# Gathers of routed rows a tile sooner, uncleared sums, and a reordered opening in a fused feedforward, attention, feedforward kernel

## The reference

```python
x = x + 0.5 * ffn(layernorm(x), ...)
x = x + attention(layernorm(x), Wk, Wq, Wv, Wo, bo)
x = x + 0.5 * ffn(layernorm(x), ...)      # the same weights again
```

## Time and profile before

| | us |
|---|---|
| median of 3 runs | 1111.91 |
| lowest and highest run | 1110.63, 1115.58 |
| profiled execution, its own time | 1111.67 |
| span of the profiled execution | 1109.9 |
| PE, DVE, ACT, POOL busy in it | 1065.2, 739.2, 552.7, 534.1 |

### The profile page before, as it was taken

How to read it: one execution, slowest core, us unless ns; L and a number is a source line. 1 busy time by engine, 2 the same in 40 slices (tenths; PEclk the granted TensorE clock), 3 DMA queues, 4 the chain that set the end, 5 groups by cost and what they waited for, 6 DMA issues and landing times.

```text
span 1109.9 us, 29561 instructions
## 1 busy us (share of the span) xinstructions
PE 1065.2 (96%) x11263; PEld 847.4 (76%) x11264; DVE 739.2 (67%) x1392; ACT 552.7 (50%) x920; POOL 534.1 (48%) x746
## 2 busy tenths in 40 slices
PE   8999999999999989999999999999999999999996
PEld 6788887888876767767767776768888877888864
DVE  5736766677654686877878778756347666767752
ACT  4344335666654456455456365343443355666641
POOL 5720554676665553462552541326201826666652
PEclk9999999999999999999999999999999999999999
DMA  7273035232224210000000000105241152422232
GB/s 267 76 265 154 19 128 178 71 127 70 74 91 143 91 57 3 3 4 2 3 3 3 2 4 3 41 2 211 90 174 39 53 186 71 132 69 70 67 111 79
DMA packets 41172, 89.77 MB, mean 81 GB/s; under 512 B 5844, under 2 KB 30551, under 8 KB 40032
## 3 DMA queue, kind: packets, MB, share of 16 engines
q1 hardware_dynamic: 30416, 62.68, 15.9%
q0 software_dynamic: 10368, 25.19, 7.3%
q10 hardware_dynamic: 272, 0.26, 0.1%
HBM read 65.04 MB, written 26.21 MB: 82 GB/s over the span
## 4 chain that ended last, share of the span: by engine, by line
PE 73%; DVE 13%; ACT 5%; issue 4%; DMA 2%; POOL 2%; DVEq 0%; ACTq 0%; POOLq 0%
PE PS L2018 14%; PE PS L1929 11%; PE PS L2032 9%; PE PS L1945 7%; PE PS L2025 3%; PE PS L2157 3%; PE PS L1860 2%; PE PS L2044 2%; PE PS L2277 2%; PE PS L2290 2%; DVE A_NM L941 2%; PE PS L1963 2%; ACT XNT L1434 1%; PE PS L2311 1%; DVE A_NM L948 1%
## 5 line engine op out<-in xcount | busy, mean ns | idle before, releaser
L2018 PE MATMUL PS<-WHL,XGH 128*128 128x512 f32 x528 | 183.4, 429 | 0.6 <-DVE WHL L802 0.6
L1763 POOL TENSOR_TENSOR A_W<-A_XC,CB 128x256 f32<-128x256 f32 x86 | 61.5, 734 | 156.0 <-DVE A_XC L1046 155.8
L2032 PE MATMUL PS<-WD,XNT 128*128 x528 | 127.2, 384 | 0.6 <-DVE HSB L861 0.6
L1330 ACT ACTIVATE XNT<-PS,SCORES 128x512 f32<-128x512 f32 x72 | 49.6, 688 | 143.2 <-PE PS L2018 127.0
L1663 POOL TENSOR_SCALAR XNTR<-WD 128x128 fp32r<-128x128 f32 x64 | 53.8, 859 | 129.5 <-DVE WD L667 129.5
L1669 POOL DMA_INDIRECT X<-xs_dram,WHO x72 | 90.6, 1259 | 46.6 <-issue 20.2
L2018 PEld LDWEIGHTS PS<-WHL,XGH 128*128 128x128 f32 x528 | 94.7, 190 | 17.5 <-issue 1.5
L1945 PE MATMUL PS<-SDH,HHL 128*128 128x256 f32 x512 | 103.4, 286 | 3.7 <-DVE X L730 3.6
L2032 PEld LDWEIGHTS PS<-WD,XNT 128*128 128x128 f32 x528 | 95.5, 190 | 13.8 <-issue 2.5
L2018 PE MATMUL PS<-WHL,XGL 128*128 128x512 f32 x264 | 104.7, 397 | 0.0
L1291 ACT CAST HHL<-HSB 128x512 fp32r<-128x512 f32 x64 | 39.7, 620 | 111.6 <-PE PS L1945 62.8
(11 more groups left out here) (312 smaller groups left out, 2613.0 us busy)
## 6 DMA issues: line engine op xcount, KB each, us to landing
xs_dram<-WG SPq DMA_DIRECT2D x16, 512.0 KB, 3.0
WU<-in_r_up SPq DMA_DIRECT2D x2, 4096.0 KB, 14.0
shared_dram<-X SPq DMA_DIRECT2D x16, 512.0 KB, 3.3
WG<-in_r_gate SPq DMA_DIRECT2D x2, 4096.0 KB, 17.9
WD<-in_r_down SPq DMA_DIRECT2D x4, 2048.0 KB, 7.7
X<-in_x SPq DMA_DIRECT2D x7, 512.0 KB, 9.3
X<-mid_dram SPq DMA_DIRECT2D x7, 512.0 KB, 3.8
X<-in_r_gate SPq DMA_DIRECT2D x6, 512.0 KB, 3.7
```

Source lines behind the costliest of these rows:

```text
L1330: act.activation(B["RS"][:, u * F:(u + 1) * F], banks[1 + u % 2][:], ACT.Silu, scale=B["SCORES"][:, bass.ds(t if tile is None else tile, 1 ...
L1763: pool.tensor_tensor(B["W"][:].rearrange("p (a m) -> p a m", m=M)[:, part, :], B["XC"][b % 2][:].rearrange("p (a w) -> p a w", w=XW)[:, pa ...
L2018: ins = pe.matmul(banks[bank][:], tok, w[:, k * F:(k + 1) * F], start=(k == 0 and i == 0), stop=(k == KD - 1 and i == 2))
L2032: ins = pe.matmul(banks[7][:, 0:D], B["HT"][:, u * F + f * P:u * F + (f + 1) * P], B["WD"][:, bass.ds(ex * (KF * D) + f * D, D)], start=(f ...
```

## The change

In the order of the code:

- `STATS_SLOT` of feedforward 0: the statistics of group 2 move from slot 0 to slot 1.
- The warm-up has 10 products in place of 8, and three more follow the turn of the first rows.
- DVE makes the low part of the shared up weights before the low parts of the first tokens, and the low part of the down weights in slot 0, after the multiplication, in place of ahead of slot 0.
- In slot 2 of feedforward 0, PE's down products come before the turn of group 1.
- In slot 28 the table is read before the low part of the hidden rows, and in the same slot the numbers of the first two experts are read earlier on DVE and ACT.
- The sums' buffer `RY` is not cleared; POOL waits for the last low part of the shared hidden rows (`hl`) in place of the clearing.
- In the routed loops DVE and ACT read one expert number at the head and one in each tile, in place of four at the head.
- POOL gathers tile 5's rows ahead of the first residual gathers, and from then on tile t + 5's rows where it gathered tile t + 4's.
- In the attention's opening, POOL normalises `S2` of batch 0 before it adds the biases, and adds batch 1's bias in the loop's first step; PE fills with 8 products in place of 3, and makes the second quarter of the maxima's scores ahead of the turned scores.

```diff
@@ -180,7 +180,7 @@
                    ht_sb=SLOT_TILES, ry_ready=SLOT_TILES, ry=SLOT_TILES, ry_out0=16 * TILES3, ry_out1=16 * TILES3, ry_out2=16 * TILES3, wg=16 + 16 * UNR, wu=16 + 16 * UNR, wd=32 + 16 * UNR,
-                   x_out=16 * PARTS_G, x_out_last=16 * (NG - PARTS_G), ry_clear=1, res_in0=16 * TILES3, res_in1=16 * TILES3, res_in2=16 * TILES3)
+                   x_out=16 * PARTS_G, x_out_last=16 * (NG - PARTS_G), res_in0=16 * TILES3, res_in1=16 * TILES3, res_in2=16 * TILES3)
     s = {k: sem(f"ffn_{k}") for k in FFN_PER}
@@ -208,7 +208,7 @@
     SEEDS = (1, FFN_PER["seed"])
-    STATS_SLOT = [{0: 2, 2: 3, 3: 4, 4: 5, 5: 6, 7: 7}, {3: 7}]
+    STATS_SLOT = [{1: 2, 2: 3, 3: 4, 4: 5, 5: 6, 7: 7}, {3: 7}]
     TURN_SLOT = {1: 2, 2: 4, 3: 6, 4: 8, 5: 9, 6: 10, 7: 11}
@@ -217,7 +217,7 @@
     TABLE_SLOT = 28
-    WARM = 8
+    WARM, WARM_TURNED = 10, 3
     GATE_BANK, UP_BANK = (0, 5), (1, 6)
@@ -563,13 +563,11 @@
                 dve.tensor_copy(SUH[:], SU).then_inc(s_split_up, 1)
-                first_low(n)
                 wait_alone(s_split_up, 1)
                 dve.tensor_tensor(SUL[:], SU, SUH[:].bitcast(F32), ALU.subtract).then_inc(s_split_up, 1)
+                first_low(n)
                 dve.wait_ge(s_x[1], 16)
                 stats(1, n)
-                dve.wait_ge(s_split_hi, 2)
-                dve.tensor_tensor(SDL[:], SD, SDH[:].bitcast(F32), ALU.subtract).then_inc(s_split_up, 1)

@@ -735,6 +733,9 @@
                     dve.tensor_tensor(hidden, hidden, banks[UP_BANK[f % 2]][:], ALU.mult).then_inc(s["h"], 1)
+                    if n == 0 and slot == 0:
+                        dve.wait_ge(s_split_hi, 2)
+                        dve.tensor_tensor(SDL[:], SD, SDH[:].bitcast(F32), ALU.subtract).then_inc(s_split_up, 1)
                     if n == 1 and slot == 0:
@@ -743,6 +744,10 @@
                         low_tile(0, 0)
+                    if slot == ROUTING_SLOT["read_table"]:
+                        read_table()
+                    if last and f == 0:
+                        ex.extend(expert(u) for u in range(2))
                     need(dve, "hh", g * KF + f + 1)
@@ -759,7 +764,6 @@
                             need(dve, "wu", 16)
-                            ex.extend(expert(u) for u in range(2))
                         low_weights(*(("WG", ex[0], 0, 0), ("WU", ex[0], 1, 1), ("WG", ex[1], 2, 2))[f])
@@ -789,8 +793,6 @@
                         find_experts()
-                    elif slot == ROUTING_SLOT["read_table"]:
-                        read_table()

@@ -848,8 +850,8 @@
                 low_weights("WU", ex[u + 1], 2 * t + 3, (2 * u) % 3)
-                if first:
-                    dve.memset(B["RY"][:], 0.0).then_inc(s["ry_clear"], 1)
+                if len(ex) < u + 3:
+                    ex.append(expert(t + 2))
                 if not first:
@@ -869,7 +871,7 @@
             with dve.Fori(1, TILES3 - UNR) as it:
-                ex = [None] + [expert(it * UNR + u) for u in range(1, UNR + 2)]
+                ex = [None, expert(it * UNR + 1)]
                 for u in range(UNR):
@@ -1285,6 +1287,9 @@
                         xgt(0, 0)
+                    if last and f == 0:
+                        need(act, "expert_of", 1)
+                        ex.extend(expert(u) for u in range(2))
                     need(act, "h", slot + 1)
@@ -1299,9 +1304,7 @@
                             need(act, "wu", 16)
-                            need(act, "expert_of", 1)
                             need(act, "x_out", 16 * PARTS_G)
-                            ex.extend(expert(u) for u in range(2))
                         high_weights(*(("WG", ex[0], 0), ("WU", ex[0], 1), ("WG", ex[1], 2))[f])
@@ -1686,19 +1691,19 @@
                 gather(u, u)
-            for u in range(2):
+            for u in range(UNR):
                 need("xg_t", u + 1)
                 gather(UNR + u, u)
+            need("hl", KF * NG)
             need("x_out", 16 * PARTS_G)
             need("x_out_last", 16 * (NG - PARTS_G))
-            need("ry_clear", 1)
             for u in range(UNR - 1):
...
                 u, ahead = t % UNR, t + UNR - 1
-                if 0 < t < SLOT_TILES - UNR - 1:
-                    need("xg_t", t + 2)
-                    gather(t + UNR + 1, (t + 1) % UNR)
+                if 0 < t < SLOT_TILES - UNR - 2:
+                    need("xg_t", t + 3)
+                    gather(t + UNR + 2, (t + 2) % UNR)
                 scatter(t, u)
@@ -1792,15 +1797,16 @@
             batch_normalise(1)
+            s2_normalise(0)
             add_bias(0)
-            add_bias(1)
-            s2_normalise(0)
             batch_root(2)
...
                 old, nxt, far, ln = b - 1, b + 1, b + 2, b + 3
+                if b == 0:
+                    add_bias(1)
                 if exists(far):
@@ -1868,10 +1874,13 @@

+            def zeros(times):
+                for _ in range(times):
+                    pe.matmul(banks[7][:, 0:NT * E], B["OH"][:, 0:P], B["OH"][:], start=True, stop=True)
+
             if n == 0:
                 pe.wait_ge(s["nobody"], 1)
-                for _ in range(WARM):
-                    pe.matmul(banks[7][:, 0:NT * E], B["OH"][:, 0:P], B["OH"][:], start=True, stop=True)
+                zeros(WARM)
                 pe.wait_ge(s_const, 16)
@@ -1904,6 +1913,7 @@
                 first_turn(n)
+                zeros(WARM_TURNED)

@@ -1977,6 +1987,9 @@
                     project(NG - 1, 1, 2)
+                turn_behind = n == 0 and slot == 2
+                if turn_behind:
+                    shared_down(0, 0)
                 if slot in turns:
@@ -1995,7 +2008,7 @@
                     xt(0, 0)
-                if slot >= 2:
+                if slot >= 2 and not turn_behind:
                     shared_down((slot - 2) // KF, (slot - 2) % KF)
@@ -2354,7 +2367,7 @@
             turn(1, 1)
-            fill(1, 3)
+            fill(1, 8)
             pe.wait_ge(att["s3m"], count("s3m", 0, 4))
@@ -2365,11 +2378,11 @@
             project_qk(1, 0)
+            pe.wait_ge(att["s1m"], count("s1m", 0, 1))
+            first_s1_max(1)
             pe.wait_ge(s_picks, 5)
...
             s3_turned(0, 0)
-            pe.wait_ge(att["s1m"], count("s1m", 0, 1))
-            first_s1_max(1)
             project_qk(1, 1)
```

## The result

| | before | after |
|---|---|---|
| median of the runs, us | 1111.91 (five, 1105.38 to 1115.58) | 1102.55 (five, 1098.29 to 1104.80) |
| ratio, with 95% interval | | 0.991 (0.9887 to 0.9933) |
| profiled execution: own time, span, us | 1111.67, 1109.9 | 1098.29, 1096.5 |

The profiled execution is the fastest of its five, so the traces differ by more (13.4 us of span) than the medians. The five runs of before in this comparison reach lower than the three shown with it.

The account below looks back on a forecast made before the run. It took TensorE, busy 1065.2 of 1109.9 us, as the bound, with only its pauses and slow stretches to win. −5.2 − 0.3 − 1.15 + 0.2 = −6.45 took 1111.9 to 1105.5 us; range 1102.6 to 1109.5.

Parts of the forecast that it names:

- Gathers: Routed parts: earlier gathers remove both pauses at tile 5's rows and the clock dip behind the second; −5.2 us.
- rival B: Clock dip behind the gathers was one execution's luck, so only the pauses go and the opening costs; 1108.7 us, chance 0.15.
- Clearing: Routed start of feedforward 1: without clearing the sums' rows the 0.62 us pause may go; half taken, −0.3 us.
- Table: Slot 28: table read ahead of the low part, covered by ACT, and PE does not wait for first gathers; 0.
- Number loads: Routed loops: one load per tile on DVE and ACT, same count, covered by PE's own work; 0.
- Rival D: Number load between two steps of every looped tile delays the low weights past PE's need; 1130 us, chance 0.05.
- Opening: Kernel's start: clock dip does not come, −1.6, and the chain of DVE and ACT loses 0.45; −1.15 us.
- Rival A: Opening keeps its clock dip, so it costs +0.45 us; 1107.0 us, chance 0.22.
- Attention's opening: Attention's start: five more fills lengthen the chain, the maxima's second product gives some back; net about +0.2 us.

Follow-up runs that it names:

- u_gather: The changed kernel with tile 5's gather and all later ones back in their old place in the order; 1105.87 us, 0.9950 of before (chip 12).
- b_loads: The kernel before with only the number loads spread; 1110.34 us, 0.9993 of before (chip 0).
- before_again: The kernel before, unchanged, measured and profiled a second time; 1111.65 us, 0.9999 (chip 0).
- b_gather_2: The kernel before with the earlier gathers alone, run again on chip 0; 1110.33 us, 0.9998 of before.
- u_loads: The changed kernel with four number loads back in the loops' heads and none in the tiles; 1096.28 us, 0.9862 of before (chip 12).
- l_att: u_loads with the attention's opening as it was before; 1103.18 us, 0.9929 of before (chip 0).
- l_clear: u_loads with the clearing of the sums' rows put back; 1103.09 us, 0.9927 of before (chip 0).
- u_loads_2: The same kernel as u_loads, run again on chip 0; 1103.56 us, 0.9926 of before.
- a_mid: The changed kernel with tile 5's gather sooner but the two-tile lead taken only from tile 9; 1096.98 us, 0.9887 of before (chip 0).
- l_mid: u_loads with tile 5's gather sooner but the two-tile lead taken only from tile 9; 1096.70 us, 0.9877 of before (chip 0).
- l_warm: u_loads with 8 warm-up products ahead of the first turn and none behind it, as before; 1106.33 us, 0.9938 of before (chip 0).
- after_again: The changed kernel, unchanged, measured and profiled a second time; 1099.18 us, 0.9883 of before (chip 0).
- u_loads_act: The changed kernel with ACT's number loads back in the loop's head and DVE's spread; 1100.70 us, 0.9900 of before (chip 0).
- l_turn: u_loads with the turn of group 1 in slot 2 ahead of the down product again; 1102.22 us, 0.9925 of before (chip 0).
- b_gather: The kernel before with the earlier gathers alone, clearing kept; 1101.51 us, 0.9908 of before (chip 12).

## Why the prediction was wrong by 3 us

Two steps of the sum failed: 1, which took the pauses at tile 5 for all that late gathers cost (−5.2; 9.1 us measured where nothing was lost), and 3, whose cover was only argued (0; −2.2 measured). Two terms are missing from it, −2.4 us in the attention and 3 to 6 us given back in the loops' first passes. The −9.4 us is what these leave together. Step by step:

1. **Gathers.** The pauses went (−1.70, −1.92) as the step says. The dip behind the second one was in three of the four profiles of kernels with late gathers (before, u_gather, b_loads; not before_again), so rival B was a quarter right. The step failed where it took these two pauses for all that late gathers cost: it looked for PE's waits in the table and found only tile 5's. The lateness of every third looped tile, 4 us in all, lay in the timeline. And it priced the earlier traffic only against the store, never against the sequencers: on chip 0 that costs 3 to 12 us in the first passes (last column). Without the loss, the part is worth 9 us; with it, the same kernel, b_gather_2, gained nothing.
2. **Clearing.** −0.3 forecast, and about right. The 2.98 us stall is absent after, and so is the 0.62 us pause. In feedforward 1 the second period is 0.57 to 0.88 us too long in all six profiles of kernels that clear, and in ten of the thirteen that do not clear and gather tile 5 early it is not too long at all (0.40 to 0.62 in after, u_loads and l_att). l_clear against u_loads_2 gives 0.15 and 0.6 us.
3. **Table.** Forecast 0, measured −1.3 and −0.95. "ACT is their cover" was argued, not read: DVE and ACT both read numbers in that slot before, and PE's waits for DVE at the shared down products (3.6 us in five) had two of 1.18 and 0.93 at this slot. I had looked only at whether PE waits for the gathers. Which of the two moves in that slot took the waits away is open.
4. **Number loads.** Forecast 0, and alone it is 0. Beside early gathers on chip 0, the three kernels that spread them on one engine or both lost 3.0 to 3.6 us (5.6 in the changed kernel's first profile), the six with all loads in the heads 4.3 to 11.7. The medians on chip 0 agree: the changed kernel took 1099.18 (in its first runs, on a chip not recorded, 1102.55), the two with half of the loads spread 1098.60 and 1100.70, the five of the changed kernel's relatives with all in the heads 1102.22 to 1106.33. So there the spread loads help, by about 4 us, and no reason was found; a_mid and l_mid, where nothing is lost, are equal. Rival D did not come. The Trainium skill's floor for such a load (DMA: Bandwidth & Descriptors, § Latency and other measured facts, about 600 ns) stays disproved by the 306 ns.
5. **Opening.** −1.15 forecast, −1.0 to −1.5 measured, for a wrong reason: I gave the whole gain to the clock and said of the move behind the down product that the chain sets the end. POOL's rows set it, and the move is what lets the clock count. Rival A's price (dip stays, +0.45) was near: l_warm has +0.2.
6. **Attention's opening.** +0.2 forecast, +0.23 seen, at the edge of what can be told.
7. **Not in the sum at all:** the attention, about −2.4 us, of which 1.9 is PE's pauses at the loading of its program. No run was made to shift that program and nothing else in the attention, but l_warm comes near, and it loses the gain.

The sum with the measured terms, at no loss: −1.3 (opening) −2.2 (slot 28) −3.6 (pauses) −1.2 (dip, three times in four) −4 (looped tiles) −0.3 (clearing) +0.2 −2.4 = −14.8; u_loads measured −14.3 against before's median. Less the 3.0 and 5.6 us lost in the first passes it is −11.8 and −9.2; the medians of after_again and after lie −12.7 and −9.4 from before's. That these agree so well is partly luck: the losses are read in profiled executions, and those two took 8.8 and 13.4 us less than before's. The range was too narrow above all because every term of it was a known pause or its absence.

What the loss is, was not settled. The three engines stop within 4 us of each other, in the first two passes of DVE's and ACT's loops, on a releaser that the profile can't name. In the changed kernel's first profile DVE had just made its first jump back. In after_again it had not; the loop was entered at 912.9 and first jumped back at 930.8, and DVE's silence begins at 919.89 (its timeline, then the chain):

```profile
924.51 0.75 DVE L849 SCALAR_TENSOR_TENSOR XNT<-PS,SCORES,XNT 128x512 f32<-128x512 f32 x1 [4.62 <-remote]
```
```profile
919.89 4.43 another core or an unknown queue
```

u_loads_act, u_loads_2 and l_turn also have a silence of 3 us ahead of DVE's first jump. PE's loop holds six tiles, not three as in the loops of DVE and ACT, and PE stopped at 201.6 in u_loads_2 where its first jump back is at 218.7. The Trainium skill (Runtime: NRT & Kernel Launch, § Instruction fetch mechanics) says that a taken branch whose target is not in the window of loaded code forces a fetch by DMA before execution goes on. That would fit the silences at a jump and the dependence on DMA traffic, but not these others; and no instruction packet is recorded in the changed kernel's trace between 195.3 and 219.1 us, so no run here shows it. Why the loss came on one chip and not on the other, was not tried further.

## What to carry to other kernels

Read a loop as a row of periods, not as one typical pass: a fifth of a microsecond in every third tile is below the table of waits and was worth as much as the two pauses that stood in it (4.0 and 3.6 us). Look into the DMA packets when a pause has no cause: here a packet of instructions had landed just before PE went on in 48 of 50. Before a wait is called covered, look up who waits for the engine at that very slot. And measure a change that moves traffic or code on more than one chip: the same kernel (b_gather) was 0.9% faster on one and no faster on the other.

## What was not expected of the hardware

- The first two passes of a loop cost 0 to 6.9 us of PE's time, with DVE and ACT silent for 2 to 5 us and PE for up to 3.9, only with gathers two tiles ahead and, in two kernels run on both chips, only on one of them.
- PE stood still for 0.5 to 1.7 us at places of its program that moved when products were added at its start, and went on 1.2 to 1.6 us after a 16 KB packet of instructions had landed.
- A granted clock back at full speed can be worth nothing: PE then waits for POOL (2.46 us) in place of working slowly.
- The clock's dips of 3.4 us (0.50 to 0.53, nearly the level of 1.2 GHz) came and went between profiles of one kernel (before: at 13, 621 and 925 us; before_again: at 13 and 740).
